# Another order of the work inside a head, on all engines, in the second phase of a two-layer transformer kernel

## The reference

```python
x = x + jnp.tanh(g_xattn[0]) * _L0_xattn_ref(_layernorm(x), ctx_2048)    # fp8-quantised product
x = x + jnp.tanh(g_ffn[0]) * _L0_ffn_ref(_layernorm(x), weight, norm)    # 8-bit rows, ternary weight
x = x + jnp.tanh(g_xattn[1]) * _L1_xattn_ref(_layernorm(x), ctx, ctx)    # attention over 8 heads
x = x + jnp.tanh(g_ffn[1]) * _L1_ffn_ref(_layernorm(x), router_w, Wa, Wb)  # 8 experts, top 2
```

## Time and profile before

| | |
|---|---|
| median of 3 runs | 2047.13 us (2046.15 to 2052.06) |
| the profiled execution | 2047.11 us, its span 2045.3 us |
| PE busy | 1859.9 us, 91% of the span |
| DVE, ACT, POOL busy | 1542.8, 1269.0, 775.0 us (75, 62, 38%) |
| granted TensorE clock, mean | 0.98 of full speed |
| mean of one `exp` (868), its bias (860) | 1.205, 0.290 us |
| mean of one `prob_high` (881), `prob_low` (1575) | 1.149, 1.283 us |
| mean of one `row_maxima` (1570) | 1.207 us |
| `turn_probs`, from issue to landing | 4.5 us median |

### The profile page before, as it was taken

The page is one execution under the profiler, slowest core; times in us unless marked ns, Lnnn a source line. Parts: engine busy times, 40 slices in busy tenths (PEclk is TensorE's granted clock), DMA queues, the critical chain, the costliest instruction groups (busy, mean ns, idle before and its releaser), DMA issues.

```text
span 2045.3 us, 26459 instructions
## 1 busy us (share of the span) xinstructions
PE 1859.9 (91%) x8968; PEld 838.5 (41%) x8968; DVE 1542.8 (75%) x2386; ACT 1269.0 (62%) x2045; POOL 775.0 (38%) x1100
## 2 busy tenths in 40 slices
PE   1699999983799999999999999999999999999998
PEld 0244444331244444444444444444444444444443
DVE  8899999887777777777777777777777777777662
ACT  4799898655555665665665555665656565565650
POOL 3556565333333333333333333333333333333320
PEclk9999999997799999999999999999999999999998
DMA  9587877795788788888878888788878878887672
GB/s 212 159 213 200 217 208 186 187 233 167 143 157 161 149 164 167 163 159 168 160 159 167 164 163 159 150 167 162 159 161 164 169 157 161 163 171 160 125 147 58
DMA packets 923975, 340.50 MB, mean 166 GB/s; under 512 B 849728, under 2 KB 898880, under 8 KB 923840
## 3 DMA queue, kind: packets, MB, share of 16 engines
q1 hardware_dynamic: 923840, 338.81, 78.8%
HBM read 93.36 MB, written 33.55 MB: 62 GB/s over the span
## 4 chain that ended last, share of the span: by engine, by line
DVE 21%; ACT 20%; issue 19%; POOL 10%; PE 7%; DMA 5%; SPq 1%; ACTq 0%; DVEq 0%; POOLq 0%
ACT slot L881 9%; DVE tiny L1570 7%; ACT arena L868 6%; POOL tiny L707 5%; DVE tiny L1216 4%; POOL tiny L705 4%; DVE slot L1575 3%; ACT tiny L860 3%; DMA slot<-slot 2%; DVE arena L1585 2%; DMA probs<-slot 2%; ACT slot L905 2%; DVE slot L1543 2%; PE accs L1059 1%; PE accs L1060 1%
## 5 line engine op out<-in xcount | busy, mean ns | idle before, releaser
L1575 DVE SCALAR_TENSOR_TENSOR slot<-arena,tiny,slot 128x1024 f16<-128x1024 f32 x256 | 328.2, 1283 | 304.2 <-ACT slot L881 304.0
L881 ACT ACTIVATE slot<-arena,tiny 128x1024 f16<-128x1024 f32 x256 | 294.2, 1149 | 173.1 <-POOL tiny L707 158.1
L1079 PE MATMUL sc<-arena,slot 128*128 128x512 f16 x1536 | 372.3, 382 | 20.9 <-ACT arena L868 18.5
L705 POOL TENSOR_SCALAR tiny<-tiny 128x1 f32<-128x1 f32 x256 | 101.0, 394 | 687.0 <-ACT arena L868 687.0
L1570 DVE TENSOR_REDUCE tiny<-sc 128x1 f32<-128x1024 f32 x256 | 306.6, 1207 | 17.5 <-PE sc L1079 16.2
L868 ACT ACTIVATE arena<-sc,tiny,head_tab 128x1024 f32<-128x1024 f32 x256 | 308.6, 1205 | 8.5
L860 ACT ACTIVATE tiny<-tiny,head_tab 128x1 f32<-128x1 f32 x256 | 74.3, 290 | 346.0 <-DVE tiny L1570 346.0
L1079 PEld LDWEIGHTS sc<-arena,slot 128*128 128x128 f16 x1536 | 150.2, 98 | 207.2 <-ACT arena L868 21.2
L1100 PE MATMUL accs<-probs,arena 128*128 128x512 f16 x512 | 195.9, 383 | 18.9 <-issue 16.4
L1059 PE MATMUL accs<-wa_both,slot 128*128 128x512 f16 x512 | 196.6, 384 | 0.0
L1060 PE MATMUL accs<-wa_both,slot 128*128 128x512 f16 x512 | 196.6, 384 | 0.0
(11 more groups left out here) (212 smaller groups left out, 2902.9 us busy)
## 6 DMA issues: line engine op xcount, KB each, us to landing
arena<-in_x SPq DMA_DIRECT2D x32, 512.0 KB, 4.2
x_scratch<-arena SPq DMA_DIRECT2D x32, 512.0 KB, 3.7
slot<-x_scratch SPq DMA_DIRECT2D x32, 512.0 KB, 4.0
slot<-in_ctx SPq DMA_DIRECT2D x32, 512.0 KB, 4.2
out<-arena SPq DMA_DIRECT2D x31, 512.0 KB, 3.4
slot<-in_L_ffn_Wa SPq DMA_DIRECT2D x12, 512.0 KB, 4.7
slot<-in_L_ffn_Wb SPq DMA_DIRECT2D x9, 512.0 KB, 5.0
wb_hi<-in_ctx SPq DMA_DIRECT2D x64, 64.0 KB, 2.4
```

Source lines behind the costliest of these rows:

```text
L881: act.activation(high, full, ACT.Identity, scale=rinv[c % 4][:]).then_inc(s_ph.sem, 1)
L1079: mm = pe.matmul(sc[:, c % 2, h * HALF:(h + 1) * HALF], q[i][:, c * P:(c + 1) * P], k[j][:, h * HALF:(h + 1) * HALF], start=start, stop=stop)
L1575: dve.scalar_tensor_tensor(out=low, in0=full, scalar=rinv[c % 4][:], in1=high, op0=ALU.mult, op1=ALU.subtract).then_inc(s_pl.sem, 1)
```

## The change

Every engine keeps its instructions; only their order inside a turn differs. The diff is cut to the loops' changed parts.

```diff
@@ sync @@
                 if cur:
+                    turn_probs(n, 0)
+                if quant:
+                    load_x1(n + 2)
+                if cur:
+                    turn_probs(n, 1)
+                if prev:
+                    turn_rows(n - 1)
+                if quant:
+                    load_k(n + 2)
+                if cur:
+                    turn_probs(n, 2)
                     turn_keys(n)
-                    turn_probs(n, 0)
-                if is_x(n + 2) and n >= -1:
-                    load_k(n + 2)
...
+                if cur:
                     turn_probs(n, 5)
+                    turn_probs(n, 6)
                 if prev and cur:
                     turn_hidden(n - 1)
-                if cur:
-                    turn_probs(n, 6)
@@ gpsimd @@
                     row_factor(n, 1)
+                if prev:
+                    ln_factors(n - 1, l4_st, l4_p, mv4, a4, rs4, nb4)
+                if cur:
+                    row_factor(n, 2)
                 if nxt:
                     query_low(n + 1)
                 if prev:
-                    ln_factors(n - 1, l4_st, l4_p, mv4, a4, rs4, nb4)
-                if cur:
-                    row_factor(n, 2)
-                if prev:
                     row_norm(n - 1)
                 if cur:
                     row_factor(n, 3)
                     row_factor(n, 4)
+                    row_factor(n, 5)
                 if prev and cur:
                     hidden_low(n - 1, 0)
                 if cur:
-                    row_factor(n, 5)
                     row_factor(n, 6)
@@ scalar @@
                 if cur:
+                    exp(n, 1)
                     prob_high(n, 0)
-                    exp(n, 1)
+                    prob_high(n, 1)
                 if nxt:
                     query_full(n + 1)
-                if cur:
-                    prob_high(n, 1)
+                if prev:
+                    rows_full(n - 1)
+                    rows_high(n - 1)
+                if cur:
+                    exp(n, 2)
                 if nxt:
                     query_high(n + 1)
-                if cur:
-                    exp(n, 2)
-                if prev:
-                    rows_full(n - 1)
-                    rows_high(n - 1)
...
@@ tensor @@
                 if cur:
                     scores(n, 0)
+                    scores(n, 1)
                 if nxt:
                     ternary(n + 1)
-                if cur:
-                    scores(n, 1)
...
                 if before:
-                    output(n - 2, 1, every)
+                    output(n - 2, 1, early)
                 if cur:
                     scores(n, 4)
+                if before:
+                    output(n - 2, 1, late)
+                if cur:
                     scores(n, 5)
                 if prev:
                     router(n - 1)
-                    hidden(n - 1, 0, every)
+                    hidden(n - 1, 0, early)
+                if cur:
+                    scores(n, 6)
+                if prev:
+                    hidden(n - 1, 0, late)
                     hidden(n - 1, 1, early)
                 if cur:
-                    scores(n, 6)
+                    scores(n, 7)
                 if prev:
                     hidden(n - 1, 1, late)
                 if cur:
-                    scores(n, 7)
                     values(n, 0, every)
@@ vector @@
                 if nxt:
                     key_low(n + 1)
-                if cur:
-                    prob_low(n, 1)
                 if prev:
                     finish_x3(n - 1, 1)
                     stats_x3(n - 1, 1)
                 if cur:
+                    prob_low(n, 1)
                     row_maxima(n, 2)
+                if prev:
+                    rows_low(n - 1)
+                if cur:
+                    row_maxima(n, 3)
                 if before:
                     finish_x4(n - 2, 0)
-                if cur:
-                    row_maxima(n, 3)
-                if prev:
-                    rows_low(n - 1)
...
                 if prev:
                     route(n - 1)
                 if cur:
+                    row_maxima(n, 5)
                     prob_low(n, 4)
                 if prev:
                     weigh_hidden(n - 1, 0)
                 if cur:
-                    row_maxima(n, 5)
                     row_maxima(n, 6)
```

More of the change, by code:

```diff
@@ L534, in _ @@
                 if cur:
-                    turn_keys(n)
                     turn_probs(n, 0)
-                if is_x(n + 2) and n >= -1:
+                if quant:
[5 more added lines that the diff above has]
+                if quant:
                     load_k(n + 2)
                 if cur:
-                    turn_probs(n, 1)
-                if is_x(n + 2) and n >= 1:
-                    load_x1(n + 2)
-                if prev:
-                    turn_rows(n - 1)
-                if cur:
                     turn_probs(n, 2)
+                    turn_keys(n)
                     turn_probs(n, 3)
-                if before and n - 2 < TILES - 1:
-                    store_out(n - 2)
                 if quant:
@@ L553, in _ @@
                     turn_probs(n, 4)
+                if before and n - 2 < TILES - 1:
+                    store_out(n - 2)
+                if cur:
                     turn_probs(n, 5)
+                    turn_probs(n, 6)
                 if prev and cur:
                     turn_hidden(n - 1)
-                if cur:
-                    turn_probs(n, 6)
             for h in range(2):
@@ L725, in _ @@
                     row_factor(n, 1)
-                if nxt:
-                    query_low(n + 1)
                 if prev:
@@ L731, in _ @@
                     row_factor(n, 2)
+                if nxt:
+                    query_low(n + 1)
                 if prev:
@@ L943, in _ @@
                 if cur:
+                    exp(n, 1)
                     prob_high(n, 0)
-                    exp(n, 1)
+                    prob_high(n, 1)
                 if nxt:
                     query_full(n + 1)
-                if cur:
-                    prob_high(n, 1)
-                if nxt:
-                    query_high(n + 1)
-                if cur:
-                    exp(n, 2)
                 if prev:
@@ L956, in _ @@
                     rows_high(n - 1)
+                if cur:
+                    exp(n, 2)
+                if nxt:
+                    query_high(n + 1)
                 if cur:
@@ L961, in _ @@
                     exp(n, 4)
-                if prev:
-                    router_exp(n - 1)
                 if cur:
@@ L966, in _ @@
                 if prev:
-                    hidden_high(n - 1, 0)
+                    router_exp(n - 1)
                 if cur:
@@ L972, in _ @@
                 if prev:
+                    hidden_high(n - 1, 0)
+                if cur:
+                    prob_high(n, 6)
+                if prev:
                     hidden_high(n - 1, 1)
                 if cur:
-                    prob_high(n, 6)
                     exp(n, 7)
@@ L1192, in _ @@
                     router(n - 1)
-                    hidden(n - 1, 0, every)
-                    hidden(n - 1, 1, early)
+                    hidden(n - 1, 0, early)
                 if cur:
@@ L1197, in _ @@
                 if prev:
+                    hidden(n - 1, 0, late)
+                    hidden(n - 1, 1, early)
+                if cur:
+                    scores(n, 7)
+                if prev:
                     hidden(n - 1, 1, late)
                 if cur:
-                    scores(n, 7)
                     values(n, 0, every)
@@ L1684, in _ @@
                     output_low(4)
+                if cur:
+                    row_maxima(n, 1)
                 if nxt:
@@ L1687, in _ @@
                 if cur:
-                    row_maxima(n, 1)
                     prob_low(n, 0)
@@ L1709, in _ @@
                 if cur:
+                    row_maxima(n, 4)
                     prob_low(n, 3)
@@ L1712, in _ @@
                     quantise_round(n + 2)
-                if cur:
-                    row_maxima(n, 4)
                 if before:
```

## The result

The changed kernel takes 2115.66 us (2109.96 to 2117.18, 4 runs), the one before, beside it, 2046.64 (2045.12 to 2052.06, 4 runs): 1.033 times as long, interval [1.031, 1.035]. In the profiled executions the span went from 2045.3 to 2113.3 us, +68.0. The forecast was 2090, with a range of 2012 to 2125.

The account below looks back on a forecast made before the run. PE was taken to bound the kernel, leaving only its gaps to win. Gaps of 0.45 + 2.5 + 0.15 + 0.3 = 3.4 us a turn against 1.93, over 29 turns, add 43 to 2047.1: 2090, range 2012 to 2125.

Parts of the forecast that it names:

- The router's wait goes: PE ahead of the router matmul: rows land at 17.5, before the router is due at 18.1, so 1.37 us goes.
- scores(4): PE waits for chunk 2's exponential, now behind rows_high on ACT: new wait of 0.45 us a turn.
- scores(6): PE waits for chunk 4's exponential, late through POOL and DVE holding each other: new wait of 2.5 us a turn.
- The rival without any exclusion: POOL and DVE don't hold each other, chunk 4 is done before 21.1: 2000 us; chance of faster 0.23.
- the one with POOL alone held: DVE isn't held by query_low, only POOL by DVE: chunk 4's wait 1.6 us, 2063 us in all; chance 0.10.
- What is late after that: Later part of a turn: 0.15 us wait for chunk 5's exponential, 0.3 left ahead of the value product's second half.
- the gap ahead of the value product: PE ahead of the value product's second half, waiting for chunk 7's transpose: 0.3 us a turn left.
- SP's moves cost nothing by this walk: SP's queue of DMA issues: its reordered transposes and loads were claimed to add no time.
- the other two score waits: PE's waits for the exponentials of chunks 4 and 5: 2.5 and 0.15 us a turn.
- The clock: PE's clock after the new 2.5 us wait: taken as staying full, as after a 2.60 wait; up to 44 us otherwise.
- the likeliest case's own range: Whole kernel, forecast as worked out without a fall of the clock: 2075 to 2105 us, chance 0.47.
- the rival with the clock: PE's clock falls in the new wait: forecast plus 15 to 44 us, 2105 to 2134; chance 0.11.

Follow-up runs that it names:

- m_port2: A kernel of its own in which only POOL and DVE meet, 24 times in each of six cases; DVE's 1.28 us instruction takes 3.03 behind POOL's 2.12.
- f2_pe_before: Changed kernel with plain copies for transposing DMAs, and TensorE's order put back as before: 2120.44 us, 1.037 of the kernel before.
- f3_norm_behind: Changed kernel with plain copies for transposing DMAs, and POOL's row_norm moved behind row_factor(3): 2050.77 us, 1.0036 of the kernel before.
- f1_pe_only: Kernel before with plain copies for transposing DMAs, given TensorE's new order alone: 2156.09 us, 1.055 of the kernel before.

## Why the prediction was right, and where it was off

*The router's wait goes.* Right. `finish_x3(1)` starts at 5.38 (1338.43 - 1333.05; worked out 5.35), its third factor ends at 9.3 (9.35), and no turn waits.

*`scores(4)`.* 0.29 against 0.45: chunk 2's bias starts at 11.57, as worked out (11.7).

*`scores(6)`.* Right in size and cause: 2.48 against 2.5. `prob_low(2)` took 2.11, `row_norm` ended at 20.2 (20.4), `prob_high(3)` started at 21.2 (21.3). The rival without any exclusion is refuted by `m_port2` and by turn n = 30; the one with POOL alone held, by the 2.11 and the 3.03.

*The first term that failed is in "What is late after that"*, where 0.3 a turn were left for the gap ahead of the value product and nothing for the second expert product. The text named one cause (`hidden_high` and `hidden_low` one call later) and asked only what chunk 7's transpose would gain; it did not ask who waits for `hidden_low`. That is `turn_hidden` and, behind it, the second expert product: 0.47 a turn, over 28 turns 13 us. "SP's moves cost nothing by this walk" failed with it: the walk left out that `turn_hidden` now stands behind `turn_probs(6)`, and it is issued 1.0 us after its input is ready. The value product's gap is 0.11 instead of 0.3, which gives back 5 us; `scores(4)`, with the hundredths of the other two score waits, another 5.

*The clock*, taken as nothing, is the largest miss: 0.61 a turn, 17 us. The argument was that a wait of 2.5 is nearest to the row of 2.60, at which the clock stayed; at 2.48 it fell in 11 of 28 turns. (The 1.5 us lost behind the wait of 2.88 are 3 us spent at half speed, and not "1.5 us at the lower" level; the price of 1.5 a fall stands, with 1.6 measured.) Since a fall hides waits behind it, the turns with one are only 0.9 longer than the nine shortest, some 10 us in all. The first turn's 3.1 us and 1.7 at the end were counted as nothing, 5 either way.

Together 13 - 5 - 5 + 17 + 5 = 25, less the 1.5 that the 29th turn was given: 23.5 of the 25.7 us between forecast and result; the rest is remainders and rounding. That the new wait and the two given back nearly cancel (13 against 10) is luck. The time lies outside the likeliest case's own range (2075 to 2105) and inside that of the rival with the clock (2105 to 2134, chance 0.11), near its lower end, as its 15 to 44 us go from ten falls to one in every turn.

*What the sum hid.* It was a sum of waits, each against a due time counted from the start of a turn. It came out near, but as a way to think it is wrong: it says that without the wait at `scores(6)` a turn would be 2.5 shorter, and `f2_pe_before` shows none of that. The wait there, and the one ahead of the expert product, are two readings of the same lateness in `row_factor(3)`: with that put right in `f3_norm_behind`, the wait is 1.6 shorter and the turn 1.7. Likewise the change's two halves don't add: alone they cost 5.9% and 4.1% (1.055 and 1.037 against 0.996), together 3.3%.

What stays open: whether the changed kernel with real transposes gains as much from moving `row_norm` (not tried); what SP's old place for `turn_hidden`, or a `query_low` of a few columns, would give (no run of either); why some landings come 1 to 2 us late; and why the clock falls in one turn and not in the next with the same wait.

## What to carry to other kernels

Where DVE reads both inputs from SBUF, count a queue of tiny POOL instructions beside it by its neighbours, not by its 0.2 us each: three in a row ahead of a factor that others need made it 2.4 us late here, and moving them gave 1.7 us a turn back. Look too at what an issuing queue puts ahead of the transfer that matters. And check a forecast made of waits against the loops of the schedule: follow each moved producer to its consumer in the next turn, since taking away one wait is worth nothing where another loop of the same length lies behind it.

## What the hardware showed that was not expected

A POOL instruction of one column can be held through two DVE instructions in a row: 1.85 us in `f3_norm_behind`, from 1353.42 to 1355.27, beside `quantise_full`'s 1353.17 to 1354.44 and 1354.48 to 1355.23. A fall of the clock came behind PE's wait of 2.5 us in 11 of 28 turns (changed kernel), behind one of 2.9 to 4.4 in 16 of 28 (`f2_pe_before`), and in 21 of 28 in `f1_pe_only` (20 behind one of 2.2, one behind a router wait of 1.9), with waits of one length on either side of the divide. In `f3_norm_behind` it fell in 2 of 28 turns, both behind a late landing's wait of 2.2 to 2.3, and not behind two others of 2.2; none of its waits of 0.9 was followed by one.
